# RWKV recurrence in a kernel of four layers: TensorE forms the keys' difference from the running peak in a PSUM bank, by a second key product and a negative identity, and the peak scan reads the keys from a bank

## The reference

```python
xx = jnp.pad(x, ((0, 0), (1, 0), (0, 0)))[:, :-1]      # the row before
xk = x * time_mix_k + xx * (1 - time_mix_k)            # xv, xr alike
k = einsum('btc,dc->btd', xk, key_w)                   # v, r alike
# per channel, over time, from aa = bb = 0, pp = -1e38, with w = -exp(time_decay), u = time_first
ww = u + k_t;  p = max(pp, ww)
y = (exp(pp-p) * aa + exp(ww-p) * v_t) / (exp(pp-p) * bb + exp(ww-p))
p2 = max(pp + w, k_t)
aa = exp(pp+w-p2) * aa + exp(k_t-p2) * v_t
bb = exp(pp+w-p2) * bb + exp(k_t-p2);   pp = p2
# result: (sigmoid(r) * y) @ output_w.T
```

## Time and profile before

| what | value |
|---|---|
| median of 3 runs | 3393.95 us (3393.68 to 3396.66) |
| profiled execution, its own time | 3394.4 us |
| its span | 3392.6 us |
| busy in the span | TensorE 3145.8, VectorE 2083.9, ScalarE 1592.4, GpSimd 1034.5 us |
| projections of the recurrence | 1989.4 to 2242.6 us of the span |

### The profile page before, as it was taken

The page is one execution under the profiler, slowest core; times in us unless marked ns, Lnnn a source line. Parts: engine busy times, 40 slices in busy tenths (PEclk is TensorE's granted clock), DMA queues, the critical chain, the costliest instruction groups (busy, mean ns, idle before and its releaser), DMA issues. The chain is left out here.

```text
span 3392.6 us, 63210 instructions
## 1 busy us (share of the span) xinstructions
PE 3145.8 (93%) x15962; PEld 2449.1 (72%) x15965; DVE 2083.9 (61%) x3584; ACT 1592.4 (47%) x2095; POOL 1034.5 (30%) x772
## 2 busy tenths in 40 slices
PE   7989999999799799999999958978998999999996
PEld 6745555555577699999999923435777999999995
DVE  4266666663685366666666649987654666666663
ACT  2224444444311266566665646623123566565663
POOL 0010001100111245445445524432122444445453
PEclk9969999999899899999999978988998999999998
DMA  5331111230301367777776530123015777776765
GB/s 174 116 71 39 39 40 39 45 95 1 120 29 51 96 159 170 174 167 170 184 177 164 108 125 4 46 100 126 22 47 157 180 173 180 173 172 171 170 137 110
DMA packets 140188, 383.51 MB, mean 113 GB/s; under 512 B 21728, under 2 KB 22496, under 8 KB 136416
## 3 DMA queue, kind: packets, MB, share of 16 engines
q1 hardware_dynamic: 86880, 252.66, 24.4%
q0 software_dynamic: 52608, 127.69, 19.6%
q10 hardware_dynamic: 576, 1.57, 0.2%
HBM read 281.42 MB, written 104.63 MB: 114 GB/s over the span
## 5 line engine op out<-in xcount | busy, mean ns | idle before, releaser
L1628 POOL DMA_INDIRECT acc_rows<-g_y,first_ids_out x232 | 520.3, 2243 | 658.9 <-DMA acc_rows<-g_y,first_ids_out 450.8
L1735 DVE TENSOR_TENSOR first_lo<-first_raw,first_hi x232 | 562.8, 2426 | 104.7 <-ACT first_hi L1676 103.5
L595 DVE TENSOR_REDUCE b_part_max<-b_p_ring 128x1 f32<-128x512 f32 (+3 forms) x640 | 359.9, 606 | 226.5 <-PE b_p_ring L682 140.3
L1676 ACT ACTIVATE first_hi<-first_raw x232 | 469.6, 2024 | 28.2 <-DMA first_raw<-in_expert_weights_dram 12.5
L569 ACT ACTIVATE b_probs<-b_p_cols 128x1024 f32<-128x1024 f32 (+1 forms) x320 | 269.2, 893 | 320.1 <-PE b_p_cols L700 320.1
L1728 DVE TENSOR_TENSOR g_hidden<-g_gate,g_p_up 128x352 f32<-128x352 f32 x232 | 121.0, 522 | 480.6 <-PE g_p_up L1797 476.5
L1795 PE MATMUL g_p_gate<-first_hi,g_rows_hi 128*128 x928 | 322.3, 347 | 19.4 <-issue 19.4
L1687 ACT ACTIVATE g_y<-g_p_y,first_rows_in 128x512 f32<-128x512 f32 x232 | 159.6, 688 | 332.3 <-PE g_p_y L1813 315.3
L1796 PE MATMUL g_p_gate<-first_lo,g_rows_hi 128*128 x928 | 302.8, 326 | 0.0
L1797 PE MATMUL g_p_gate<-first_hi,g_rows_lo 128*128 x928 | 301.9, 325 | 0.0
L1795 PE MATMUL g_p_up<-first_hi,g_rows_hi 128*128 x928 | 298.2, 321 | 0.0
(11 more groups left out here) (326 smaller groups left out, 6474.8 us busy)
## 6 DMA issues: line engine op xcount, KB each, us to landing
first_raw<-in_expert_weights_dram SPq DMA_DIRECT2D x248, 544.0 KB
acc_rows<-f_acc SPq DMA_DIRECT2D x34, 256.0 KB, 2.0
qk_hi<-a_hi SPq DMA_DIRECT2D x32, 256.0 KB, 2.6
qk_lo<-a_lo SPq DMA_DIRECT2D x32, 256.0 KB, 2.9
xn_rows<-f_xn SPq DMA_DIRECT2D x8, 1024.0 KB, 5.2
b_q_stack<-qk_hi SPq DMA_DIRECT2D x28, 256.0 KB
b_k_stack<-qk_hi SPq DMA_DIRECT2D x28, 256.0 KB
first_raw<-in_expert_weights_dram SPq DMA_DIRECT2D x2, 2176.0 KB, 8.9
```

The lines of the kernel that those rows point to most:

```text
L595: v.tensor_reduce(part_max[:, h, t % BT, c:c + 1], p_ring[:, ring, 0:w], AX.X, ALU.max).then_inc(rows_free, 1)
L1628: pool.indirect_dma_start(out=acc_rows, out_offset=bass.IndirectOffsetOnAxis(ap=ids_out[:, i:i + 1].bitcast(U32), axis=0), in_=y[:, n, :], ...
L1676: act.activation(hi[:, bass.ds(place, PIECE)], raw[:, bass.ds(source, PIECE)], ACT.Copy).then_inc(split_hi_ready, 1)
L1735: v.tensor_tensor(lo[:, bass.ds(place, PIECE)], raw[:, bass.ds(source, PIECE)], hi[:, bass.ds(place, PIECE)].bitcast(F32), ALU.subtract).t ...
```

## The change

The key product goes to a bank of its own, `p_k`, and is not copied: the peak scan reads the bank. `delta` and `kk` are gone from SBUF. The difference is now formed in a third bank, `p_delta`: a new step of TensorE, `subtract_peak(n)`, repeats the four matmuls of the key product there and adds a fifth, the peaks' row of `state` times `neg_ident`, a negative identity that VectorE makes once at the start. The fifth waits for the scan (`peak_ready`), the first of them until `past_now(n - 1)` has read the bank (`e_ready`). ScalarE reads the difference from the bank four times. To make room, `p_mm` shrinks from three banks to one, which values and receptance share: the value product waits for the copy of the receptance of unit n-1, the receptance product for the copy of the values of unit n. ScalarE's copies of values and receptance now stand ahead of `keep_take` in a unit.

```diff
@@ -1872,10 +1872,9 @@
         w_neg = sb("w_neg", [P, KD])
         u = sb("u", [P, KD])
         u_neg = sb("u_neg", [P, KD])
-        kk = sb("k", [P, 2, BW])
+        neg_ident = sb("neg_ident", [P, P])
         vv = sb("v", [P, NV, BW])
         er = sb("er", [P, NV, BW])
-        delta = sb("delta", [P, 2, BW])
         kt = sb("kt", [P, 2, 2, BW])
         e = sb("e", [P, NV, 2, BW])
         ev = sb("ev", [P, 2, BW])
...
@@ -1886,7 +1885,9 @@
         x_add = sb("x_add", [P, BT, D])
         norm = Norm(k, "r_norm", s)
         p_turn = s.enter_context(nc.psum_tensor("r_p_turn", [P, BW], F32))
-        p_mm = s.enter_context(nc.psum_tensor("r_p_mm", [P, 3, BW], F32))
+        p_k = s.enter_context(nc.psum_tensor("r_p_k", [P, BW], F32))
+        p_delta = s.enter_context(nc.psum_tensor("r_p_delta", [P, BW], F32))
+        p_mm = s.enter_context(nc.psum_tensor("r_p_mm", [P, BW], F32))
         p_out = s.enter_context(nc.psum_tensor("r_p_out", [P, BT, D], F32))
 
         def sem(what):
...
@@ -1950,7 +1952,7 @@
                     if n >= 1:
                         fraction_top(n - 1)
                     pool.wait_ge(kt_ready, n + 1)
-                    pool.wait_ge(copied, 3 * n + V_ + 1)
+                    pool.wait_ge(copied, 2 * n + V_)
                     if n >= 2:
                         pool.wait_ge(scans_done, 2 * (n - 1))
                     chain.link(pool.tensor_tensor(ev[:, n % 2, :], kt[:, n % 2, 1, :], vv[:, n % NV, :], ALU.mult))
...
@@ -1985,34 +1987,30 @@
 
                 def copy_product(n, j):
                     act.wait_ge(product, 3 * n + j + 1)
-                    if j == K_:
-                        if n >= 2:
-                            act.wait_ge(delta_ready, n - 1)
-                        act.activation(kk[:, n % 2, :], p_mm[:, j, :], ACT.Copy).then_inc(copied, 1)
-                    elif j == V_:
+                    if j == V_:
                         if n >= NV:
                             act.wait_ge(top_ready, n - NV + 1)
-                        act.activation(vv[:, n % NV, :], p_mm[:, j, :], ACT.Copy).then_inc(copied, 1)
+                        act.activation(vv[:, n % NV, :], p_mm[:], ACT.Copy).then_inc(copied, 1)
                     else:
                         if n >= NV:
                             act.wait_ge(y_ready, n - NV + 1)
-                        act.activation(er[:, n % NV, :], p_mm[:, j, :], ACT.Exp, scale=-1.0).then_inc(copied, 1)
+                        act.activation(er[:, n % NV, :], p_mm[:], ACT.Exp, scale=-1.0).then_inc(copied, 1)
 
                 def keep_take(n):
                     c = n % KD
                     act.wait_ge(delta_ready, n + 1)
                     if n >= 2:
                         act.wait_ge(scans_done, 2 * (n - 1))
-                    chain.step(act.activation(kt[:, n % 2, 0, :], delta[:, n % 2, :], ACT.Relu, bias=w_neg[:, c:c + 1]))
-                    chain.link(act.activation(kt[:, n % 2, 1, :], delta[:, n % 2, :], ACT.Relu, bias=w[:, c:c + 1], scale=-1.0))
+                    chain.step(act.activation(kt[:, n % 2, 0, :], p_delta[:], ACT.Relu, bias=w_neg[:, c:c + 1]))
+                    chain.link(act.activation(kt[:, n % 2, 1, :], p_delta[:], ACT.Relu, bias=w[:, c:c + 1], scale=-1.0))
                     act.activation(kt[:, n % 2, :, :], kt[:, n % 2, :, :], ACT.Exp, scale=-1.0).then_inc(kt_ready, 1)
 
                 def past_now(n):
                     c = n % KD
                     if n >= NV:
                         act.wait_ge(y_ready, n - NV + 1)
-                    chain.step(act.activation(e[:, n % NV, 0, :], delta[:, n % 2, :], ACT.Relu, bias=u[:, c:c + 1]))
-                    chain.link(act.activation(e[:, n % NV, 1, :], delta[:, n % 2, :], ACT.Relu, bias=u_neg[:, c:c + 1], scale=-1.0))
+                    chain.step(act.activation(e[:, n % NV, 0, :], p_delta[:], ACT.Relu, bias=u[:, c:c + 1]))
+                    chain.link(act.activation(e[:, n % NV, 1, :], p_delta[:], ACT.Relu, bias=u_neg[:, c:c + 1], scale=-1.0))
                     act.activation(e[:, n % NV, :, :], e[:, n % NV, :, :], ACT.Exp, scale=-1.0).then_inc(e_ready, 1)
 
                 norm.scalar_root(act, 0)
...
@@ -2027,21 +2025,20 @@
                 for n in range(UNITS):
                     b, c = n // KD, n % KD
                     ahead = b + 1 < NB
-                    copy_product(n, K_)
                     if ahead and c < 2:
                         copy_rows(b + 1, 2 * c)
+                    copy_product(n, V_)
+                    if ahead and c < 2:
+                        copy_rows(b + 1, 2 * c + 1)
+                    copy_product(n, R_)
                     if ahead and c >= 2:
                         scale_rows(b + 1, c - 1)
                     keep_take(n)
-                    copy_product(n, V_)
-                    if ahead and c < 2:
-                        copy_rows(b + 1, 2 * c + 1)
                     if ahead and c == 1:
                         scale_rows(b + 1, 0)
                     if ahead and c >= 1:
                         scale_shifted(b + 1, c - 1)
                     past_now(n)
-                    copy_product(n, R_)
                     if b + 2 < NB and c == 2:
                         norm.scalar_root(act, b + 2)
...
@@ -2071,11 +2068,8 @@
 
                 def advance_peak(n):
                     c = n % KD
-                    v.wait_ge(copied, 3 * n + K_ + 1)
-                    chain.link(v.tensor_tensor_scan(state[:, PP_, c, 1:BW + 1], w[:, c:c + 1].to_broadcast([P, BW]), kk[:, n % 2, :], state[:, PP_, c, 0:1], ALU.add, ALU.max))
-                    if n >= 2:
-                        v.wait_ge(e_ready, n - 1)
-                    v.tensor_tensor(delta[:, n % 2, :], kk[:, n % 2, :], state[:, PP_, c, 0:BW], ALU.subtract).then_inc(delta_ready, 1)
+                    v.wait_ge(product, 3 * n + K_ + 1)
+                    v.tensor_tensor_scan(state[:, PP_, c, 1:BW + 1], w[:, c:c + 1].to_broadcast([P, BW]), p_k[:], state[:, PP_, c, 0:1], ALU.add, ALU.max).then_inc(peak_ready, 1)
 
                 def sums(n):
                     c = n % KD
...
@@ -2090,7 +2084,7 @@
                     v.wait_ge(e_ready, n + 1)
                     chain.link(v.tensor_tensor(below[:], e[:, n % NV, 0, :], state[:, BB_, c, 0:BW], ALU.mult))
                     chain.link(v.tensor_tensor(below[:], below[:], e[:, n % NV, 1, :], ALU.add))
-                    v.wait_ge(copied, 3 * n + R_ + 1)
+                    v.wait_ge(copied, 2 * n + R_)
                     chain.link(v.scalar_tensor_tensor(below[:], er[:, n % NV, :], 1.0, below[:], ALU.add, ALU.mult))
                     chain.link(v.reciprocal(below[:], below[:]))
                     v.wait_ge(top_ready, n + 1)
...
@@ -2112,6 +2106,7 @@
                         v.wait_ge(x_add_loaded[t], 16 * (b + 1))
                         v.tensor_tensor(x_add[:, t, :], p_out[:, t, :], x_add[:, t, :], ALU.add).then_inc(out_added, 1)
 
+                v.tensor_scalar(neg_ident[:], ident, -1.0, None, ALU.mult).then_inc(neg_ready, 1)
                 chain.step(v.memset(xT[:, :, 0:1], 0.0))
                 chain.step(v.memset(state[:, PP_, :, 0:1], NEG))
                 chain.link(v.memset(state[:, BB_:AA_ + 1, :, 0:1], 0.0))
...
@@ -2172,11 +2167,26 @@
                         pe.wait_ge(w_loaded[j], 16)
                     if c == 0:
                         pe.wait_ge(mixed_ready, b * 3 + j + 1)
-                    if n >= 1:
-                        pe.wait_ge(copied, 3 * (n - 1) + j + 1)
+                    if j == K_:
+                        if n >= 1:
+                            pe.wait_ge(peak_ready, n)
+                    elif j == R_ or n >= 1:
+                        pe.wait_ge(copied, 2 * n + j - 1)
+                    dst = p_k[:] if j == K_ else p_mm[:]
                     for kc in range(KD):
-                        m = pe.matmul(p_mm[:, j, :], wkvr[:, j, kc, c * P:(c + 1) * P], mixed[:, b % 2, j, kc, :], start=(kc == 0), stop=(kc == KD - 1))
+                        m = pe.matmul(dst, wkvr[:, j, kc, c * P:(c + 1) * P], mixed[:, b % 2, j, kc, :], start=(kc == 0), stop=(kc == KD - 1))
                     m.then_inc(product, 1)
+
+                def subtract_peak(n):
+                    b, c = n // KD, n % KD
+                    if n == 0:
+                        pe.wait_ge(neg_ready, 1)
+                    else:
+                        pe.wait_ge(e_ready, n)
+                    for kc in range(KD):
+                        pe.matmul(p_delta[:], wkvr[:, K_, kc, c * P:(c + 1) * P], mixed[:, b % 2, K_, kc, :], start=(kc == 0), stop=False)
+                    pe.wait_ge(peak_ready, n + 1)
+                    pe.matmul(p_delta[:], neg_ident[:], state[:, PP_, c, 0:BW], start=False, stop=True).then_inc(delta_ready, 1)
 
                 def output(n):
                     b, c = n // KD, n % KD
...
@@ -2204,6 +2214,7 @@
                     if b + 1 < NB and c < 2:
```

(4 more changed lines are left out.)

## The result

The changed kernel takes 3455.02 us (median of 4 runs, 3451.63 to 3458.35) against 3393.81 us (median of 4, 3393.00 to 3396.66) of the kernel before it: ratio 1.0179, 95% interval 1.0161 to 1.0196. The prediction was 3455.0 in 3435 to 3486, slower with 0.97.

A forecast was written before the change was run, and what follows sets the result against it. TensorE and VectorE were both nearly full in the projections, and TensorE would become the bound everywhere. The terms 68.6 - 21.6 - 10.7 + 9.0 + 6.0 + 5.4 + 8.4 - 4.5 gave +60.6, so 3455 us, range 3435 to 3486.

The forecast's parts named there:

- More products: TensorE, every unit: five added matmuls, 80 in all at 0.858 us each, cost +68.6 us.
- The cover: TensorE's five old gaps in the projections vanish, -21.6 us, and the low clock behind them, -10.7 us.
- rival 4: Added products on TensorE are cheaper than their like in the trace: 26.6 us less, 3429 us; chance 0.02.
- Values to receptance: Receptance projection waits for the value's copy from the shared bank: 0.83 us in eight units, 0.39 in six, +9.0 us.
- Units 2 and 3: TensorE waits there for value copies queued late in ScalarE's order: gaps of 3.6 and 2.4 us, +6.0 us.
- Turns: At the turns of units 4 and 8 TensorE waits for normalized rows: 2.7 us twice, +5.4 us.
- Clock behind these four: The gaps of units 2 and 3 and both turns lower TensorE's clock: 2.1 us each, +8.4 us.
- Tail: From last projection to last output add: 23.8 us instead of 28.3, as VectorE has caught up, -4.5 us.
- the short gap: Rival: the short value-to-receptance gaps also lower TensorE's clock, 29 us more, 3484 us; chance 0.08.
- The round trip: Rival: the path from difference through ScalarE and VectorE to the peak becomes the bound, +10 us, 3465; chance 0.07.
- all new waits hide: Rival: only TensorE's added work, cover and tail count, +31.8 us, 3426 us; chance 0.03.
- the added products fit into TensorE's free time: Rival: VectorE's chain stays the pace and its relief of 22.0 us comes through, 3372 us; chance 0.02.

The follow-up runs named there:

- the work alone: The kernel before with five more key matmuls per unit into the same bank, no wait, bank or order changed: 3423.11 us, ratio 1.0088.
- one repeat: The changed kernel with one of the four repeated key matmuls kept per unit, waits and order unchanged: 3426.65 us, ratio to before 1.0089.
- the identity products: The changed kernel with the four repeated matmuls replaced by one, identity times keys that ScalarE copies to SBUF: 3423.83 us, ratio to before 1.0089.
- the subtraction alone on the bank: The kernel before, keys still copied and scanned from the copy, only VectorE's subtraction reading them from the bank: 3387.79 us, ratio 0.9973.

## Why the prediction was right

Point by point, each against the trace of the changed kernel:
- **More products, +68.6.** Right: 3.43 us for four and 0.86 for the fifth.
- **The cover, -21.6 and -10.7.** Right for the five gaps: they are gone both from the kernel with the work alone, whose stream cost +31.1 us, and from the changed kernel. The changed kernel and the one before have a sixth, in unit 0, which I counted on neither side; up to the end of the first value product that unit took 1.3 us more than before, which is within its wander.
- **The Trainium skill's 131 ns.** It would have made 3429. Four repeated matmuls measured 0.858 us each, 214 ns for each of the four passes that the prediction counts, so the figure of the page "TensorE: Matmul & The Clock Gate" (Back-to-back issue gap) does not hold for these float32 products, and rival 4 falls.
- **Values to receptance, +9.0.** Under-sized: a gap costs 0.85, as priced, and then 0.11 more (2117.47 to 2121.01 is 3.54 for 3.43), a slow restart that I left out. With a turn between, 2078.16 to 2082.61 less the turn's 0.44 and the product's 3.43 leaves 0.58. 8 x 0.96 + 6 x some 0.55 = 11.0.
- **Units 2 and 3, +6.0.** Right: 3.4 and 2.4 (2037.74 and 2056.56, less 3.43 from the starts before them), the mechanism as described: ScalarE's order.
- **Turns, +5.4.** 2.98 each, 6.0.
- **Clock behind these four, +8.4.** The step that was mis-sized: I gave all four the price of the old gaps. Two ran at 0.67 and cost 1.8 and 1.7 us, two at 1.00 and cost nothing: +3.5. Even that is the figure of one execution: behind the gap of unit 2 (3.2 to 3.7 us) four matmuls took 1.8 us too long in the changed kernel, 3.1 with one repeat (2039.31 to 2045.87) and 0.1 with the identity products (2036.38 to 2039.91).
- **Tail, -4.5.** Half right: 2327.87 - 2301.84 = 26.0 against 28.3, so -2.3. VectorE had caught up as told, but the last two scans took nearly twice the 1.26 us of the earlier trace rows. VectorE's timeline at the first of them, the second (at 2306.74) takes 2.32 us too:

```profile
2304.50 2.32 DVE L2077 TENSOR_TENSOR_SCAN r_state<-r_kt,r_state 128x512 f32<-128x512 f32 x1 [4.70 <-ACT r_kt L2006]
```

The errors are +2.0 and +0.6 for the gaps and turns, -0.2 for units 2 and 3, -4.9 for the clock, +2.2 for the tail and +1.3 for unit 0: +1.0 in sum, where the measured total is off by only +0.1; the remaining -0.9 is in no term that I can name. The errors cancel: the mechanism was right, but that the total came out to 0.1 us was luck.

Of the rivals, the short gap did not lower the clock: a steady unit's 18.98 us are 21 matmuls at 0.858, 18.02, and one gap of 0.96, and the granted clock of those units, 2165 to 2300, is 1.00. But the row that I held against this rival was weaker than it looked. The 1.64 us gap of the earlier trace rows is one of several of its kind; behind another of 1.64 us in the same trace, at 2329.34, the granted clock was 0.50 from 2330.43 to 2333.41. The round trip was not the bound, since no wait of TensorE for the peak stands in the trace. That all new waits hide is refuted by the 31.1 us between the work alone and the whole change, and that the added products fit into TensorE's free time by the 29.6 us that they cost alone.

## What to carry to other kernels

When an engine that is nearly full is relieved by another that is nearly full too, price the work added against the idle time that the second engine really has, clock losses included; here 68.6 us met 32.3, and 37.5 where it stood early enough to cover unit 0 as well. Then walk the new order unit by unit, since half of the loss was not work but where it stood: gaps from a shared bank, a copy queued behind steps that wait, and old gaps that the new work came too late to fill. And look for the half of the change that costs nothing: reading the keys from their bank, which came along with a losing idea, gave 0.3% alone.

## What the runs showed of the hardware

- A VectorE operation with both inputs in SBUF takes longer when a GpSimd product is already running, and one that started first slows GpSimd's product instead. The subtraction takes 0.69 us alone and 1.40 to 1.58 beside GpSimd; with one input in a PSUM bank it takes 0.69 even wholly beside it. GpSimd's product, started 0.16 us into a peak scan, takes 1.98 to 2.16 us if the scan has both inputs in SBUF and 1.09 to 1.27 if it reads the bank. The scan itself stays at 1.25 to 1.28 us when it reads a bank. The Trainium skill says so on its page "SBUF — State Buffer" (SBUF: two separate sides): a VectorE operation with two SBUF inputs and a GpSimd operation that reads SBUF need the same pair of ports, and whichever starts first holds it for its whole length. The trace agrees on who is slowed and, within some 0.2 us, on how long. What I had not expected is that the lost time is handed on: with the subtraction alone on the bank L2092 took up 8.6 of the 10.9 us that the subtraction saved (20.6 against 12.0), so only VectorE's sum over all operations tells a gain.
- Gaps of TensorE of like length did not lower its clock alike: behind 3.21 us and behind one of the 2.81 us turns (2154.12) it read 0.67, between the 1.2 and the 2.4 GHz level; behind 2.27 it read 1.00, and behind the other turn four matmuls took 3.44 us, the time of the high level. Across the kernels the spread is wider: behind 3.20 us the clock read 0.53 (one repeated matmul, 2039.31 to 2045.87), behind 3.69 us 1.00 (identity products, 2036.38 to 2039.91). The length of a gap alone does not decide it, and these runs do not show what does.
- A stalled product restarts some 0.1 us late: 3.54 us for four matmuls behind each 0.69 us wait (3.51 behind 0.34 and 0.78), 3.43 otherwise.
